# Router logits of a transformer block in fp32: router weights stationary and both token parts moving, instead of token tiles stationary

## What is computed

```python
x = x + attn(_layernorm(x), queries, combiners)
x = x + xattn(_layernorm(x), ctx_1024, ctx_1024, Wq, bq, Wk, bk, Wv, bv)
# ffn of the normalised x (y2 in the kernel), N = 4096 tokens, E = 16 experts, K = 2
logits = x_tokens @ router_w + router_b          # (4096, 512) @ (512, 16)
probs = softmax(logits); vals, idx = top_k(probs, 2)
# each expert takes at most 640 tokens; expert and shared MLP: silu(h @ wg) * (h @ wu) @ wd, F = 704
out = x + shared_mlp(x_tokens) + gated sum of the two experts' outputs
```

## Time and profile before

| | us |
|---|---|
| median of 3 runs | 1950.61 (1949.41 to 1950.73) |
| the profiled execution, its own time | 1950.5 |
| its span in the profile | 1948.7 |
| one iteration of the first phase, for i = 2 to 6 (from one `G` to the next in the timeline) | 69.0 |

### The profile page before, as it was taken

The page is one execution under the profiler, slowest core; times in us unless marked ns, Lnnn a source line. Parts: engine busy times, 40 slices in busy tenths (PEclk is TensorE's granted clock), DMA queues, the critical chain, the costliest instruction groups (busy, mean ns, idle before and its releaser), DMA issues.

```text
span 1948.7 us, 27982 instructions
## 1 busy us (share of the span) xinstructions
PE 1914.9 (98%) x10832; PEld 1697.4 (87%) x10832; DVE 821.2 (42%) x1887; ACT 680.5 (35%) x1389; POOL 808.1 (41%) x661
## 2 busy tenths in 40 slices
PE   8999999999999999999999999999999999999997
PEld 5788888888878788888799999999999999999996
DVE  2566576667574332222333333333333333343332
ACT  3344444443454211111333333333333433334321
POOL 2132144134254300001555665665655656556531
PEclk9999999999999999999999999999999999999999
DMA  8020330231144222231444554545544455444522
GB/s 277 2 95 15 109 109 23 87 109 64 57 130 151 46 44 49 49 81 25 111 125 115 134 111 97 134 119 126 120 94 128 124 120 126 98 124 125 121 31 28
DMA packets 98293, 186.66 MB, mean 96 GB/s; under 512 B 14544, under 2 KB 14544, under 8 KB 97904
## 3 DMA queue, kind: packets, MB, share of 16 engines
q1 hardware_dynamic: 72864, 131.75, 21.6%
q0 software_dynamic: 25296, 53.11, 15.2%
HBM read 127.53 MB, written 57.29 MB: 95 GB/s over the span
## 4 chain that ended last, share of the span: by engine, by line
PE 68%; DVE 1%; ACT 1%; issue 1%; POOL 0%; DMA 0%; ACTq 0%; DVEq 0%; POOLq 0%
PE ps L70 44%; PE ps L1236 22%; PE ps L1182 2%; ACT buffer L1046 0%; DVE buffer L1128 0%; PE ps L647 0%; POOL buffer L990 0%; DMA buffer<-in_wts 0%; DVE smax L550 0%; PE ps L640 0%; ACT buffer L338 0%; ACT buffer L333 0%; POOL out_tokens L1035 0%; DVE buffer L1146 0%; ACT L1091 0%
## 5 line engine op out<-in xcount | busy, mean ns | idle before, releaser
L70 PE MATMUL ps<-buffer,buffer 128*128 128x320 f32 (+1 forms) x6816 | 1243.4, 342 | 7.2 <-DVE buffer L535 2.1
L70 PEld LDWEIGHTS ps<-buffer,buffer 128*128 128x128 f32 x6816 | 1100.6, 188 | 107.3 <-issue 3.7
L990 POOL TENSOR_TENSOR buffer<-buffer,buffer 128x512 fp32r<-128x512 f32 x289 | 387.8, 1506 | 231.8 <-ACT buffer L1046 231.5
L1236 PE MATMUL ps<-buffer,buffer 128*128 128x512 f32 x1904 | 458.3, 395 | 2.1 <-DVE buffer L1128 2.1
L1236 PEld LDWEIGHTS ps<-buffer,buffer 128*128 128x128 f32 x1904 | 352.3, 189 | 74.9 <-POOL buffer L990 3.2
L1146 DVE TENSOR_TENSOR buffer<-ps,buffer 128x320 f32<-128x320 f32 (+1 forms) x240 | 127.7, 532 | 602.4 <-ACT buffer L1091 564.7
L1091 ACT ACTIVATE buffer<-ps 128x320 f32<-128x320 f32 (+1 forms) x240 | 112.5, 469 | 636.2 <-PE ps L70 617.7
L1046 ACT ACTIVATE buffer<-buffer 128x512 fp32r<-128x512 f32 (+3 forms) x561 | 286.3, 566 | 55.9 <-PE ps L1236 50.5
L1035 POOL DMA_INDIRECT out_tokens<-buffer,slot_index x80 | 125.6, 1570 | 219.7 <-DVE buffer L1171 210.3
L1128 DVE TENSOR_TENSOR buffer<-buffer,buffer 128x320 fp32r<-128x320 f32 (+1 forms) x240 | 187.7, 782 | 11.6 <-ACT buffer L1046 10.5
L305 POOL TENSOR_TENSOR buffer<-buffer,buffer 128x512 fp32r<-128x512 f32 x32 | 41.1, 1316 | 299.6 <-ACT buffer L333 299.6
(11 more groups left out here) (102 smaller groups left out, 981.2 us busy)
## 6 DMA issues: line engine op xcount, KB each, us to landing
buffer<-in_wts SPq DMA_DIRECT2D x289, 256.0 KB
buffer<-in_x SPq DMA_DIRECT2D x8, 1024.0 KB, 6.6
buffer<-in_ctxT SPq DMA_DIRECT2D x8, 1024.0 KB, 10.7
tokens_normed<-buffer SPq DMA_DIRECT2D x8, 1024.0 KB, 4.6
out_tokens<-buffer SPq DMA_DIRECT2D x8, 1024.0 KB, 4.3
tokens_normed_T<-buffer SPq DMA_DIRECT2D x8, 1024.0 KB, 8.7
buffer<-tokens_normed_T SPq DMA_DIRECT2D x8, 1024.0 KB, 7.0
out_tokens<-buffer POOLq DMA_DIRECT2D x32, 256.0 KB, 3.9
```

What stands on the lines that cost most here:

```text
L70: last = pe.matmul(out, left, right, start=(i == 0), stop=(i == len(todo) - 1))
L990: pool.tensor_tensor(wl[n % RING][:], wraw[n % RAW][:], wh[n % RING][:].bitcast(F32), ALU.subtract).then_inc(s_wl, 1)
L1236: ins = pe.matmul(down_bank[n % 2][:], left, right, start=(c == 0 and i == 0), stop=(c == FC - 1 and i == len(passes) - 1))
```

## The change

- `Y2T` now makes two parts: ACT copies the bank as the high part `y2h` (fp32r, in the place of `prob`), and DVE subtracts it from the bank to give the low part `y2l`. The bank counts as drained when DVE is done.
- `LP` replaces the 16 products: the router's weights, high part in columns 0 to 15, low part in 16 to 31 and zeros up to 128 (`rwp`), are stationary, and the 512 tokens of `y2h` and `y2l` move: 8 fp32r matmuls for a batch, behind `Q`. The logits come out with experts in partitions. ACT copies them to `logits_T`, and `LX` on PE transposes them back with four transposes into the same bank. `L` on DVE now has two additions, since high and low weights have columns of their own.
- In `order`, `LP` stands behind `Q`, `LX` behind `G`, and `L` behind `T`. In the table `router`, `LP` stands behind unit 3 and `LX` and `L` behind unit 4.
- `YT` holds both parts; SP stores and loads twice as much. The shared MLP reads them as they are (`yh`, `yl`), so the splits `TOKENS`, `x_hi` and `x_lo` are gone for groups 0 to 7. Waits that guard the buffers change with them: among them ACT's copy of `G` and its softmax of `SC` wait for both stores, and the loads wait for other semaphores.

```diff
-def three_pass(pe, out, parts, between=()):
+def three_pass(pe, out, parts):
...
         last = pe.matmul(out, left, right, start=(i == 0), stop=(i == len(todo) - 1))
-        if i % 3 == 2 and between:
-            between.pop(0)()
...
-    YT = nc.dram_tensor("tokens_normed_T", (B, D, S), F32, kind="Internal").ap()
+    YT = nc.dram_tensor("tokens_normed_T", (2, B, D, S), F32, kind="Internal").ap()
...
+    y2h = at(88, [NC, S], F32R)
+    y2l_rows = [at(8, [NC, S], F32R)] * (B - 2) + [at(38, [NC, S], F32R), at(52, [NC, S], F32R)]
...
             if name == "Y2T":
+                sp.wait_ge(s_y2h, NC * (b + 1))
+                sp.dma_start(YT[0, b].rearrange("(c p) s -> p c s", p=P), y2h[:].bitcast(F32)).then_inc(s_ytout, 16)
                 drained(sp, "Y2T", b, NC - 1)
-                sp.dma_start(YT[b].rearrange("(c p) s -> p c s", p=P), prob[:]).then_inc(s_ytout, 16)
+                sp.dma_start(YT[1, b].rearrange("(c p) s -> p c s", p=P), y2l(b)[:].bitcast(F32)).then_inc(s_ytout, 16)
...
-                    copy(prob[:, c, :], bank[:]).then_inc(s_ev["Y2T"], 1)
+                    copy(y2h[:, c, :], bank[:]).then_inc(s_y2h, 1)
+            if name == "LP":
+                filled(act, "LP", b)
+                bank = bank_of("LP", b)
+                copy(logits_T[:], bank[:]).then_inc(s_ev["LP"], 1)
...
             if name == "G":
+                if b >= 2:
+                    act.wait_ge(s_ytout, 32 * (b - 1))
...
+            if name == "Y2T":
+                for c in range(NC):
+                    dve.wait_ge(s_y2h, NC * b + c + 1)
+                    filled(dve, "Y2T", b, c)
+                    bank = bank_of("Y2T", b, c)
+                    dve.tensor_tensor(y2l(b)[:, c, :], bank[:], y2h[:, c, :].bitcast(F32), ALU.subtract)\
+                        .then_inc(s_ev["Y2T"], 1)
...
-                filled(dve, "L", b)
-                bank = bank_of("L", b, 0)
-                dve.tensor_tensor(lg[:], bank[:, 0:NT * E].rearrange("p (t e) -> p t e", e=E),
-                                  rb_all[:].unsqueeze(1).to_broadcast([P, NT, E]), ALU.add)\
-                    .then_inc(s_ev["L"], 1)
-                drained(dve, "L", b)
+                filled(dve, "LX", b)
+                bank = bank_of("LX", b)[:].rearrange("p (t m) -> p t m", m=P)
+                link(dve.tensor_tensor(lg[:], bank[:, :, 0:E], rb_all[:].unsqueeze(1).to_broadcast([P, NT, E]), ALU.add))
+                dve.tensor_tensor(lg[:], bank[:, :, E:2 * E], lg[:], ALU.add).then_inc(s_ev["LX"], 1)
+                drained(dve, "LX", b)
...
+            if name == "LP":
                 drained(pe, "Y2T", b, NC - 1)
-                for product in logit_products(b):
-                    product()
+                pe.wait_ge(s_rw, 2)
+                products = [(rwp[:, c, :], y[:, c, :]) for c in range(NC) for y in (y2h, y2l(b))]
+                f32_group(bank_of("LP", b)[:], products).then_inc(s_mm["LP"], 1)
+            if name == "LX":
+                drained(pe, "LP", b)
+                for t in range(NT):
+                    cols = slice(t * P, (t + 1) * P)
+                    last = pe.transpose(bank_of("LX", b)[:, cols], logits_T[:, cols], ident[:])
+                last.then_inc(s_mm["LX"], 1)
...
-                drained(pe, "L", b - 2)
+                drained(pe, "LX", b - 2)
...
-             "PT": [("TOKENS", 0), ("WEIGHTS", (8, FIRST))]}
+             "PT": [("WEIGHTS", (8, FIRST))]}
...
-                 ("L", i - 1), ("G", i + 1), ("T", i + 1), ("WV", i + 1), ("QB", i + 1),
+                 ("LP", i - 1), ("G", i + 1), ("LX", i - 1), ("T", i + 1), ("L", i - 1), ("WV", i + 1), ("QB", i + 1),
...
-    router = {(0, 2): [("Y2T", B - 1)], (0, 3): [("L", B - 1)], (1, 0): [("X", B - 1)]}
+    router = {(0, 2): [("Y2T", B - 1)], (0, 3): [("LP", B - 1)], (0, 4): [("LX", B - 1), ("L", B - 1)],
+              (1, 0): [("X", B - 1)]}
...
-            pe.wait_ge(s_xl, tiles_before[g + 1])
+            if job == 0:
+                pe.wait_ge(s_xn[g % 2], 32 * (g // 2 + 1))
+                x_hi, x_lo = yh[g % 2], yl[g % 2]
```

More of the change, by code:

```diff
@@ L113, in sem @@
         return ctx.enter_context(nc.semaphore(name))
-    BANK = {"Y1T": (0, 1, 2, 3), "V": (4, 5, 6, 7), "Y2T": (0, 1, 2, 3), "L": (0,), "Q": (4, 5, 6, 7),
+    BANK = {"Y1T": (0, 1, 2, 3), "V": (4, 5, 6, 7), "Y2T": (0, 1, 2, 3), "LP": (0,), "LX": (0,), "Q": (4, 5, 6, 7),
             "G": (1,), "YT": (2, 3, 4, 5), "T": (6, 7, 0, 1), "SC": (2, 3, 4, 5), "X": (6,), "M": (7,),
@@ L120, in phase1 @@
             "W": (5, 6, 7, 0), "KR": (4,), "QB": (2,)}
-    LAST_BANK = {"Y2T": (5, 6, 7, 4), "L": (4,), "X": (5,)}
+    LAST_BANK = {"Y2T": (5, 6, 7, 4), "LP": (4,), "LX": (4,), "X": (5,)}
     def bank_of(step, b, i=0):
@@ L146, in phase1 @@
     rw = sb("rw", [P, NC, E], F32)
+    rwp = sb("rwp", [P, NC, P], F32R)
+    logits_T = sb("logits_T", [P, S], F32)
     rb_all = sb("rb_all", [P, E], F32)
@@ L279, in gpsimd @@
         pool.memset(ones[:], 1.0).then_inc(s_const, 1)
+        pool.memset(rwp[:].bitcast(F32), 0.0).then_inc(s_rwz, 1)
         pool.memset(count[:], 0.0).then_inc(s_const, 1)
@@ L368, in step @@
             if name == "WV":
+                act.wait_ge(s_small, 16 * 5)
+                act.wait_ge(s_rwz, 1)
+                copy(rwp[:, :, 0:E], rw[:]).then_inc(s_rw, 1)
                 act.wait_ge(s_wv, 16)
@@ L495, in step @@
                 last.then_inc(s_wh, 1)
+                dve.wait_ge(s_rw, 1)
+                dve.tensor_tensor(rwp[:, :, E:2 * E], rw[:], rwp[:, :, 0:E].bitcast(F32), ALU.subtract).then_inc(s_rw, 1)
+            if name == "Y2T":
[5 more added lines that the diff above has]
+                        .then_inc(s_ev["Y2T"], 1)
             if name == "QB":
@@ L642, in transposes @@
             last.then_inc(s_mm[step], 1)
-        def logit_products(b):
-            def product(t, c):
-                ins = pe.matmul(bank_of("L", b)[:, t * E:(t + 1) * E], prob[:, c, t * P:(t + 1) * P], rw[:, c, :],
-                                start=(c == 0), stop=(c == NC - 1))
-                if (t, c) == (NT - 1, NC - 1):
-                    ins.then_inc(s_mm["L"], 1)
-            return [lambda t=t, c=c: product(t, c) for t in range(NT) for c in range(NC)]
         pe.wait_ge(s_const, 8)
@@ L931, in tail @@
     def tail(g):
-        after = tiles_of[g + 1] if g + 1 < NG else 0
+        after = tiles_of[g + 1] if g + 1 < NG and groups[g + 1][0] > 0 else 0
         for t in range(max(tiles_of[g], after)):
@@ L945, in load_tokens @@
             if g >= 2:
-                sp.wait_ge(s_xl, tiles_before[g - 1])
-            elif g == 1:
-                sp.wait_ge(attn["s_yout"], 16 * B)
-            sp.wait_ge(attn["s_ytout"], 16 * (g + 1))
-            sp.dma_start(xt[g % 2][:], YT[g].rearrange("(c p) s -> p c s", p=P)).then_inc(s_xn[g % 2], 16)
+                sp.wait_ge(s_gu, unit_no[(g - 2, FC - 1, 0)] + 1)
+            sp.wait_ge(attn["s_ytout"], 32 * (g + 1))
+            for part, dst in enumerate((yh[g % 2], yl[g % 2])):
+                sp.dma_start(dst[:].bitcast(F32), YT[part, g].rearrange("(c p) s -> p c s", p=P)).then_inc(s_xn[g % 2], 16)
         def load_weights(n):
@@ L1057, in x_hi @@
             cols = slice(t * P, (t + 1) * P)
-            if groups[g][0] == 0:
-                act.wait_ge(s_xn[g % 2], 16 * (g // 2 + 1))
-                copy(xh[:, :, cols], xt[g % 2][:, :, cols]).then_inc(s_xh, 1)
-                return
             n = gathered[g] + t
@@ L1075, in scalar @@
                     split(n)
-            elif name == "TOKENS":
-                for t in range(NT):
-                    x_hi(0, t)
             elif name not in ("RAW", "LOAD"):
@@ L1131, in vector @@
         for name, b in order:
-            if name == "TOKENS":
-                for t in range(NT):
-                    x_lo(0, t)
-            elif name not in ("RAW", "LOAD", "WEIGHTS"):
+            if name not in ("RAW", "LOAD", "WEIGHTS"):
                 step(name, b)
@@ L1206, in tensor @@
                             (wh[m % RING][:, d * P:(d + 1) * P], wl[m % RING][:, d * P:(d + 1) * P],
-                             xh[:, d, cols], xl[:, d, cols]) for d in range(NC)])
+                             x_hi[:, d, cols], x_lo[:, d, cols]) for d in range(NC)])
                     ins.then_inc(s_gu, 1)
@@ L1214, in tensor @@
                 if what == "x":
-                    if groups[gx][0] > 0:
-                        transpose_tile(gx, t)
+                    transpose_tile(gx, t)
                     continue
```

54 lines of the change are left out of this document (27 added, 27 removed).

## The result

The changed kernel takes **1967.85 us** (median of 4 runs, 1966.51 to 1968.9) against 1950.67 for the kernel before beside it (1949.41 to 1951.1): 17.2 us more, a ratio of 1.0089 (95% interval 1.0071 to 1.0106). Forecast were 1970, and 1958 to 1977. The profiled execution took 1968.63, its span is 1966.9.

A forecast was written before the change was run, and what follows sets the result against it. PE, busy 98%, was taken as the bound. Terms 12.1 + 0 + 0.2 - 2.7 + 3.1 gave +12.7 us, the clock +6.7: +19.4 on 1950.5, so 1970, range 1958 to 1977.

The forecast's parts named there:

- What PE saves: PE's logits: 16 products (3.51 us) become 8 matmuls (1.86) and 4 transposes (0.44), 1.21 us less a batch, 9.7 in all.
- What DVE gets: Four subtractions ahead of LN0 cost DVE 2.40 us; PE waits 2.9 and starts G 1.27 later in iterations 2 to 6.
- What LX adds: Ahead of T: LX itself 0.44 us, then PE waits 0.71 for DVE's two additions; with G's delay +12.1 over iterations 2 to 6.
- Iteration 1: G starts 1.20 us earlier, and LX's 0.44 and the 0.71 wait take that back: 0.
- Iteration 7: No G here; LX waits about 2.6 us for ACT's logits copy behind six weight splits: +0.2 us.
- Group 0: Second phase: -2.7 us from PE's saving and a clock fall gone; +3.1 from waits for down chunks 4 and 5.
- The clock: New PE gaps cost the upper clock level: five falls at 1.5 us, less 0.8 for the one at 680: +6.7 us.
- The one at 680: Existing clock fall over 680 to 685 in the kernel before; half of it was forecast to go, -0.8 us.
- the seven gaps: New PE gaps of 2.5 to 3.1 us: five before G, one before LX, one in group 0.
- No clock lost: Rival: the waits come but the gaps cost no clock; +12.7 us, 1963; chance 0.18.
- Late stores: Rival: the second store delays ACT's copy of G by 2 us in six iterations; +12 on top, 1982; chance 0.05.
- Faster: Rival: DVE's four subtractions don't delay G, so PE's saved work counts; 1939 to 1946; chance 0.07.

The follow-up runs named there:

- the kernel that beats both: Changed kernel with DVE's subtractions behind LN0, LX before the transposes, LP's high parts first, batch 7's banks, top-2, X and six weight splits moved: 1941.28 us.

## Why the prediction was right, step by step

- **What PE saves.** 16 products to 8 and four transposes: 3.5 became 636.08 - 634.25 = 1.83 and 0.44. Right; the kernel that beats both gets it.
- **What DVE gets.** 2.40 forecast, 2.39 measured; a wait of 2.9 forecast, 2.87 to 3.18 measured. The kernel before with only this load shows the wait by itself.
- **What LX adds.** `LX` to `T` is 444.61 - 443.39 = 1.22 against 0.44 + 0.71. The view names no releaser for the 0.62 ("issue"); that the wait goes when `LX` moves ahead of the transposes ties it to the draining of `LX`'s bank. Per iteration without a fall 2.52 to 2.55 against 2.42, and 5 x 2.53 = 12.7 against 12.1.
- **Iteration 1**, forecast 0: 0.05. It waits 0.45 where I had 0.4 in the sum.
- **Iteration 7**, forecast +0.2: -0.2. The wait of 2.54 for `LX` was foreseen; `PT`'s shrank from 2.25 to 1.68.
- **Group 0.** Up to the first down product -2.93 against -2.7, the fall behind the narrow products being gone as said. The wait of 2.86 is the forecast 2.9; the 0.2 for the next chunk didn't come. From the first down product to group 1 it is 4.84, and the 1.98 beside the wait lie in a stretch with a fall.
- **The clock**, forecast +6.7 from five falls at 1.5 and half of one saved. There were three: behind `G`'s gap in iterations 2 (3.1 us, twice as long as the others) and 3 (1.8), and in group 0 (2.0). The one at 680 is gone whole, -1.6. Together +5.3. This is the term that was mis-sized, by 1.4. Of the seven gaps three cost clock, not five, but each of the three cost more than the 1.5 I had, so it is partly luck that the term came this close. The kernel with the cut store, which has the same gaps, had four falls in its profiled execution.
- **The start** is 0.44 later in this execution, which nothing in the change explains: PE's first matmul, which waits for a load, starts at 8.85 instead of 8.42. The fall near 40 us, which lasts half as long in some of the other profiled executions, puts this point some 1.6 earlier there.

Sum: 0.4 + 0.05 + 12.7 - 0.2 - 2.9 + 2.9 + 5.3 = 18.2, the difference (18.1) of the profiled executions; 19.4 were forecast. By the median it is 17.2.

**The rivals.** "No clock lost" fell: three falls stand in the trace. The Trainium skill, "TensorE: Matmul & The Clock Gate", section "HAM oscillation — how this bites in real kernels", counts only gaps longer than any here, and gaps of 2.9 to 3.2, even 1.1, went with falls. "Late stores" fell with the run that cut them. "Faster" came about only when DVE's order and `LP`'s waits were changed, and its 1939 to 1946 was worked out too low: even without the subtractions `y` is there at 422.56, 0.48 behind PE's 422.08, which is up to 2.4 us in five iterations. The story of DVE was right in its number and incomplete in its cause: the row ahead of `LN0` that I read as gapless work holds a product of 2.41 us beside three of 0.68, and it lasted until POOL's additions ended.

**Open.** Why a gap costs clock in one place and not in another. One of 2.88 kept the upper level in the changed kernel, one of 2.89 in the same iteration lost it with `LX` moved, and 1.1 was enough elsewhere. So the length alone doesn't decide it in this range, and what does stays open here.

## What to carry to other kernels

Where PE is at 98%, an edit that takes work off PE and puts it on DVE has to be priced by the margin of the next wait, here 1.17 us: 1.2 us of PE's work were saved per batch and 3.5 us of waiting bought (2.88 and 0.62), 2.5 us net. A new wait costs its length and perhaps the clock behind it, so the same move can lose beside a long gap and win without one. Split a wait for a whole buffer into waits for its parts, and do the parts that are ready first.

## What the runs showed of the hardware that was not expected

- In the kernel before with DVE's load added, four gaps of 1.1 us on PE were each followed by the lower clock level (granted 0.50) and one of 1.25 wasn't; in the changed kernel three gaps of 2.87 to 2.88 kept the upper level, and those of 3.03 and 3.18 didn't.
- 32 narrow matmuls in one row, with PE never idle, were followed by a granted clock of 0.52; the same 32 in groups of eight by 1.00.
- A DVE instruction of 128x4 took 5.23 us beside four POOL additions, instead of 0.23.
